# Softmax denominators of a cross-attention kernel: one of the probability sums moved to an accumulating transfer that GpSimd issues, VectorE summing all eight probability tiles, and ones products of half the width

## The chip, the cores and the metric

One core of one Trainium2 chip runs the whole kernel. The metric is the device time of one execution in microseconds (us), as the median over several executions. Durations below are from one execution that the hardware profiler recorded.

## The reference, cut to what matters

A cross-attention layer is followed by a gated expert layer, all in float32. There are 4 batches, 512 query rows, 1024 context rows and 16 heads of width 64:

```python
q = (lat @ Wq).reshape(b, n, HEADS, DHEAD).transpose(0, 2, 1, 3)
k, v = jnp.split(ctx @ Wkv, 2, axis=-1)            # then split in heads; k is rotated (rope)
attn = jnp.einsum('bhnd,bhsd->bhns', q, k) * scale
attn = jnp.clip(attn, -11.0, 11.0)
attn = jax.nn.softmax(attn, axis=-1)
out = jnp.einsum('bhns,bhsd->bhnd', attn, v)
x = x + (out.reshape(b, n, INNER) @ Wo + bo)
sel = jax.nn.sigmoid(jnp.einsum('bsd,ed->bse', xn, expert_sel))      # xn: normalised rows of x
scores = jax.nn.relu(jnp.einsum('bsd,edh->bseh', xn, keys))
x = x + jnp.einsum('bseh,ehv,bse->bsv', scores, values, sel)
```

The change is in how the sum over the 1024 context rows under the softmax is formed. The exponentials of a head pair stand in 8 tiles of 128 context rows each. The sum over the 8 tiles, and then over the 128 partitions, gives the denominators of 2 heads x 512 queries.

## The kernel before, in words

**Stages.** `attention_phase` handles 32 head pairs (4 batches x 8 pairs) one after another in a loop `for n in range(NPAIR): iteration(n)`, which each engine runs in its own order. `ffn_phase` then handles 4 chunks of 512 rows with 16 experts each. There is no scheduler: each engine's program is written out by hand, every instruction runs in the order written, and waits on semaphores join the engines.

**One iteration on each engine.** An iteration has 4 macro steps m = 0 to 3, each of two tiles of 128 context rows (s = 2m, 2m+1). TensorE writes the scores of a tile in one of two PSUM buffers (`scores`, L905), ScalarE takes the exponential into one of 4 buffers `probs` (`exp`, L1106), and VectorE clips it in place (`clip`, L1369). TensorE then multiplies it with the values (`attend`, L918). It runs two tiles behind within a pair, so that tiles 6 and 7 of pair n are attended in macro step 0 of iteration n+1. Between these come the projections of the next pair (keys, queries, values; all `product`, L149), the projection of the output of pairs before (`project_y`, L149), and for the first 22 iterations the normalising, turning and splitting of one more context tile.

**The denominators before.** After each macro step VectorE adds the two clipped tiles into `p_sum[m]` (`sum_up`, L1378, 128 x 1024 elements). In macro step 2 it adds `p_sum[0]` to `p_sum[1]` and in macro step 0 of the next iteration `p_sum[2]` to `p_sum[3]` (`sum_quad`, L1384). TensorE multiplies the two sums with a 128 x 32 tile of ones in four products of 512 columns (`denominators`, L931), each on 32 partitions of `side_ps`: two heads x two quad sums. ScalarE copies `o_ps` to `o_raw` (L1113; it first waits for `split_o`, L213, of the pair before) and then `side_ps` to `den` (L1117). SyncE turns four rows of `den` into `den_rows` (`turn_den`, L170). VectorE adds the two halves and inverts (`invert_den`, L177 and L179, in macro step 1), SyncE stores the result in memory (`store_inv`, L185) and loads it back spread over the partitions (`spread_inv`, L192), and VectorE scales `o_raw` (`scale_o`, L200, in macro step 2, just ahead of `sum_quad`).

**Order around the change.** SyncE's queue in iteration n is: `swap_k`, from n = 2 on `load_tile`, `turn_den(n-1)`, while n + 3 < 8 `load_weights(n+3)` (three transfers, L506 and L510), `store_inv(n-1)`, `spread_inv(n-1)`, and then the packs. `load_weights(n+3)` waits until the weights of pair n+2 have been split:

```python
def load_weights(w):
    wait(sp, w_split, w)
```

That split is GpSimd's `split_weights(n+2)` (L719 to L723) in iterations 0 to 5. GpSimd's order in iteration n before the change is: `rstd` (L682), `split_weights(n+2)`, in even iterations up to 2 `split_v_weights` and in iteration 0 also `split_first`, then `split_tile` (L702 to L709).

VectorE's order in macro step 1 is: normalise, clip, rope products, clip, `sum_up(n, 1)`, `split_q`, `invert_den`, `rope_add`. In macro step 2 it is: two clips, `add_y`, `sum_up(n, 2)`, `split_k`, `scale_o`, `sum_quad(n, 0)`. In the last iteration `sum_quad(n, 0)` follows `sum_up(n, 2)` directly, without the rope, key and query work between.

Of the kernel before, what the change touches and what calls it, by code (L numbers as in the profile page):

```python
# [74 lines left out]
def shared_state(nc, st):  # L75
# [26 lines left out]
    sh.den_rows = sb("den_rows", [P, 2, NQ // DH])  # L102
# [21 lines left out]
    sh.den_added = sem("den_added")  # L124
# [38 lines left out]
def turn_den(sp, sh, n):  # L163

    wait(sp, sh.den_evac, n + 1)
    for h in range(2):
        for e in range(2):
            at = DH * h + QUAD * e
            row = sh.den[at:at + 1, :].rearrange("a (p j) -> a p j", p=DH)
            sp.dma_start(sh.den_rows[DH * h:DH * h + DH, e, :], row).then_inc(sh.den_turned, DMA)  # L170


def invert_den(dve, sh, n):

    wait(dve, sh.den_turned, 4 * DMA * (n + 1))
    wait(dve, sh.inv_stored, DMA * n)
    dve.tensor_tensor(sh.inv_rows[:], sh.den_rows[:, 0, :], sh.den_rows[:, 1, :], ALU.add).then_inc(sh.den_added, 1)  # L177
    wait(dve, sh.den_added, n + 1)
    dve.reciprocal(sh.inv_rows[:], sh.inv_rows[:]).then_inc(sh.den_inv, 1)  # L179
# [86 lines left out]
def attention_phase(nc, sh, x, ctx_in, cosT, sinT, cols, Wq, Wkv, Wo, selT, keys, values, sel_dram, packs, v_packs,  # L266
                    inv_dram):
    with ExitStack() as st:
# [126 lines left out]
        quads_up = sem("quads_up")  # L395
        pv_done = sem("pv_done")
# [273 lines left out]
        def _(pool):  # L670
# [70 lines left out]

            def head_norm(t):
# [32 lines left out]
            def iteration(n):  # L775
                t, p = n + FIRST_TILES, n + 1
                if t < TILES:
                    rstd(t)
                if n + 2 < PAIRS:
                    split_weights(n + 2)  # L780
# [17 lines left out]
        def _(pe):  # L798
# [123 lines left out]
            def denominators(n):  # L922

                pe.wait_ge(quads_up, 2 * n + 2)
# [3 lines left out]
                for e in range(2):  # L928
                    for h in range(2):
                        at = DH * h + QUAD * e  # L930
                        mm = pe.matmul(side_ps[at:at + QUAD, :], ones[:], p_sum[2 * e + 1][:, h, :],  # L931
                                       start=True, stop=True)
# [109 lines left out]
        def _(act):  # L1042
# [65 lines left out]
            def evac_o(n):  # L1108
# [8 lines left out]
                act.copy(den[:], side_ps[:]).then_inc(den_evac, 1)  # L1117
# [93 lines left out]
        def _(dve):  # L1211
# [160 lines left out]
            def sum_up(n, m):  # L1372

                dve.wait_ge(clipped, STEPS * n + 2 * m + 2)
                if m % 2 == 1:
                    wait(dve, den_ready, n)
# [3 lines left out]
            def sum_quad(n, half):  # L1380

                dve.wait_ge(summed_up, MACROS * n + 2 * half + 2)
                first, second = p_sum[2 * half], p_sum[2 * half + 1]
                dve.tensor_tensor(second[:], first[:], second[:], ALU.add).then_inc(quads_up, 1)  # L1384
# [68 lines left out]
            def iteration(n):  # L1453
                p, t = n + 1, n + FIRST_TILES
                for m in range(MACROS):
# [17 lines left out]
                    if m == 0 and n > 0:  # L1473
                        sum_quad(n - 1, 1)
# [17 lines left out]
                    if m == 2:  # L1492
                        if last:
                            sum_quad(n, 0)
# [4 lines left out]
                        if not last:  # L1499
                            sum_quad(n, 0)  # L1500
# [12 lines left out]
            sum_quad(NPAIR - 1, 1)  # L1513
# [472 lines left out]
```

## Time and profile before

| | |
|---|---|
| median of 3 executions | 1025.62 us (1022.86 to 1027.14) |
| the profiled execution, its own time | 1021.78 us |
| its span in the profile | 1019.8 us |
| busy TensorE / VectorE / ScalarE / GpSimd | 95% / 81% / 50% / 25% |
| TensorE clock granted | 1.00 in every window read |
| attention iterations | 32, the denominators of the first at 67.7 us, of the last at 821.9 us |

The span is the time from the first to the last recorded instruction. An engine's busy time counts its instructions alone. TensorE's ends are modelled, so its stages are best read from start to start. The expert layer takes the time after some 825 us and is not touched, but for the denominators of pair 31, whose last steps lie in it.

### The profile page before, as it was taken

The page shows a single profiled execution, that of the slowest core. Times are in us where ns is not written, and L with a number is a line of the kernel's source. Part 1 is how long each engine was busy: PE and PEld are TensorE (multiplying, and loading weights), DVE is VectorE, ACT ScalarE, POOL GpSimd, SP SyncE. Part 2 cuts the span into 40 slices and gives each one's busy share as a digit, 9 for nine tenths or more (in the row PEclk, how much of TensorE's full clock was granted, in tenths as well). Part 3 has the DMA queues.
Part 4 walks back from the last instruction along what each step waited for, and adds up shares of the span by engine and source line. Part 5 has one row for each costly group of instructions (what it writes and reads, how often), then busy time and mean ns, then how long its engine had stood idle before and what let it go on. Part 6 is the DMA issues. An engine that isn't in the chain of part 4 may idle for free. (4 is left out here: it accounts for less than half of the span.)

```text
span 1019.8 us, 15953 instructions
## 1 busy us (share of the span) xinstructions
PE 973.5 (95%) x5688; PEld 618.8 (61%) x5688; DVE 827.5 (81%) x1234; ACT 513.6 (50%) x727; POOL 258.3 (25%) x228
## 2 busy tenths in 40 slices
PE   3989899999999999999999999999999879999998
PEld 2745455555555555555555555555555358888898
DVE  6699889999999999999999878989888876545322
ACT  4655555565556556566555555556555532222221
POOL 3354323121212121221312100321000135445443
PEclk9999999999999999999999999999999999999999
DMA  5643323332323232232333233233222481342331
GB/s 155 199 130 102 94 84 109 100 94 69 94 68 95 79 92 90 73 89 74 95 94 93 74 94 84 84 84 83 85 63 64 128 266 52 126 122 86 112 112 46
DMA packets 68953, 100.36 MB, mean 98 GB/s; under 512 B 21968, under 2 KB 44752, under 8 KB 66832
## 3 DMA queue, kind: packets, MB, share of 16 engines
q1 hardware_dynamic: 68880, 99.41, 32.7%
q8 instruction: 43, 0.70, 0.3%
q14 instruction: 30, 0.25, 0.1%
HBM read 70.01 MB, written 10.75 MB: 79 GB/s over the span
## 5 line engine op out<-in xcount | busy, mean ns | idle before, releaser
L1106 ACT ACTIVATE wide_a<-score_ps 128x1024 f32<-128x1024 f32 x256 | 249.0, 1028 | 119.8 <-PE score_ps L905 119.6
L1369 DVE TENSOR_SCALAR wide_a<-wide_a 128x1024 f32<-128x1024 f32 x256 | 188.6, 767 | 41.5 <-ACT wide_a L1106 41.5
L1378 DVE TENSOR_TENSOR p_sum<-wide_a 128x1024 f32<-128x1024 f32 x128 | 156.6, 1223 | 2.3
L918 PE MATMUL o_ps<-wide_a,v_sb 128*64 128x512 f32 x512 | 124.2, 605 | 4.6 <-issue 2.7
L918 PE MATMUL o_ps<-wide_a,values_a 128*64 128x512 f32 x512 | 124.0, 605 | 3.8 <-DVE wide_a L1369 2.1
L905 PE MATMUL score_ps<-q_hi,k_hi 64*128 64x512 f32 x512 | 114.6, 444 | 2.8 <-DVE k_lo L1348 2.1
L1881 DVE SCALAR_TENSOR_TENSOR act<-h_ps,wide_a 128x512 f32<-128x512 f32 x64 | 44.1, 690 | 89.2 <-PE h_ps L149 83.8
L905 PEld LDWEIGHTS score_ps<-q_hi,k_hi 64*128 64x128 f32 x512 | 47.8, 183 | 112.5 <-issue 75.0
L1807 ACT CAST act_hi<-act 128x512 fp32r<-128x512 f32 x64 | 39.8, 621 | 138.1 <-DVE act L1881 138.1
L1681 POOL TENSOR_TENSOR act_lo<-act,act_hi 128x512 fp32r<-128x512 f32 x64 | 84.8, 1326 | 95.8 <-ACT act_hi L1807 95.8
L905 PE MATMUL score_ps<-q_hi,k_lo 64*128 64x512 f32 x512 | 101.1, 391 | 0.0
L905 PE MATMUL score_ps<-q_lo,k_hi 64*128 64x512 f32 x512 | 100.4, 389 | 0.0
L702 POOL CAST wide_hi<-ctx_t 128x256 fp32r<-128x256 f32 x22 | 24.9, 1131 | 225.6 <-ACT x_t L1051 120.9
L1384 DVE TENSOR_TENSOR p_sum<-p_sum 128x1024 f32<-128x1024 f32 x64 | 80.5, 1257 | 0.0
L149 PE MATMUL out_ps<-val_hi,act_hi 128*128 128x256 f32 x256 | 72.9, 285 | 0.0
L149 PE MATMUL job_ps<-wv_hi,wide_hi 128*128 128x256 f32 x240 | 70.7, 295 | 1.4 <-ACT v_sb L1092 1.4
L149 PE MATMUL out_ps<-val_hi,act_lo 128*128 128x256 f32 x256 | 71.5, 279 | 0.0
L149 PE MATMUL out_ps<-val_lo,act_hi 128*128 128x256 f32 x256 | 71.5, 279 | 0.0
L918 PEld LDWEIGHTS o_ps<-wide_a,v_sb 128*64 128x64 f32 x512 | 31.2, 136 | 62.2 <-issue 54.5
L682 POOL TENSOR_TENSOR rstd_sb<-var_sb,power 128x2 f32<-128x2 f32 x22 | 22.9, 1041 | 178.8 <-DVE var_sb L1235 109.9
L918 PEld LDWEIGHTS o_ps<-wide_a,values_a 128*64 128x64 f32 x512 | 31.2, 136 | 60.2 <-issue 55.3
L149 PE MATMUL job_ps<-wv_lo,wide_hi 128*128 128x256 f32 x240 | 67.7, 282 | 0.0
(229 smaller groups left out, 2044.1 us busy)
## 6 DMA issues: line engine op xcount, KB each, us to landing
wide_a<-sel_dram SPq DMA_DIRECT2D x16, 1024.0 KB, 4.8
k_swap<-k SPq DMA_DIRECT2D x124, 128.0 KB, 2.3
w_hi<-packs_hi SPq DMA_DIRECT2D x26, 384.0 KB, 3.1
w_lo<-packs_lo SPq DMA_DIRECT2D x26, 384.0 KB, 3.7
den<-inv_dram SPq DMA_DIRECT2D x64, 128.0 KB, 2.9
ctx_raw<-ctx SPq DMA_DIRECT2D x24, 128.0 KB, 2.2
packs_hi<-w_hi SPq DMA_DIRECT2D x8, 384.0 KB, 3.2
packs_lo<-w_lo SPq DMA_DIRECT2D x8, 384.0 KB, 3.5
```

Of the source, the lines that this page charges most:

```text
L149: mm = pe.matmul(out, lhsT, rhs, start=start and i == 0, stop=stop and i == len(terms) - 1)
L682: pool.tensor_tensor(rstd_sb[slot][:], var_sb[slot][:], power[:, 0:2], ALU.pow).then_inc(rstd_ready, 1)
L702: pool.tensor_copy(ctx_at(ctxT_hi, t), ctx_t32[:]).then_inc(tile_hi, 1)
L905: mm = pe.matmul(score_ps[s % 2][:, h, :], k[par][rows, s * P:(s + 1) * P], q[par][rows, :], start=(i == 0), stop=(i == len(terms) - 1))
L918: mm = pe.matmul(o_ps[DH * h:DH * h + DH, :], v_sb[n // 2 % 2][:, at:at + DH], probs[s % RING][:, h, :], start=(s == 0), stop=(s == STEPS ...
L1106: act.activation(probs[s % RING][:], score_ps[s % 2][:], ACT.Exp, scale=DH ** -0.5).then_inc(exp_done, 1)
L1369: dve.tensor_scalar(probs[s % RING][:], probs[s % RING][:], CLIP_HI, CLIP_LO, ALU.min, ALU.max).then_inc(clipped, 1)
L1378: dve.tensor_tensor(p_sum[m][:], first, second, ALU.add).then_inc(summed_up, 1)
L1384: dve.tensor_tensor(second[:], first[:], second[:], ALU.add).then_inc(quads_up, 1)
L1681: pool.tensor_tensor(act_lo[e % ARING][:], act32[e % ARING][:], act_hi[e % ARING][:], ALU.subtract).then_inc(act_split, 1)
L1807: act.copy(act_hi[e % ARING][:], act32[e % ARING][:]).then_inc(act_hi_done, 1)
L1881: dve.scalar_tensor_tensor(out=act32[e % ARING][:], in0=h_ps[e % HRING][:], scalar=0.0, in1=gates[:, at:at + 512], op0=ALU.max, op1=ALU.mu ...
```

## The change

The sum of the first four tiles (`p_sum[0]` into `p_sum[1]`) leaves VectorE and becomes a transfer within SBUF that adds to its destination. GpSimd issues it, between `rstd` and `split_weights`. VectorE adds that sum to `p_sum[2]` where it added the first quad (`sum_six`), and the result to `p_sum[3]` where it added the second (`sum_all`). The ones products read one sum of eight tiles, each product 256 columns of it, and ScalarE copies 256 columns of `side_ps` in place of 512. The four transfers of `turn_den` each bring 256 elements to 32 partitions in place of 512 to 64, and `invert_den` has no addition left.

```diff
@@ turn_den
-            row = sh.den[at:at + 1, :].rearrange("a (p j) -> a p j", p=DH)
-            sp.dma_start(sh.den_rows[DH * h:DH * h + DH, e, :], row).then_inc(sh.den_turned, DMA)
+            row = sh.den[at:at + 1, 0:NQ // 2].rearrange("a (p j) -> a p j", p=QUAD)
+            sp.dma_start(sh.den_rows[at:at + QUAD, :], row).then_inc(sh.den_turned, DMA)
@@ invert_den
-    dve.tensor_tensor(sh.inv_rows[:], sh.den_rows[:, 0, :], sh.den_rows[:, 1, :], ALU.add).then_inc(sh.den_added, 1)
-    wait(dve, sh.den_added, n + 1)
-    dve.reciprocal(sh.inv_rows[:], sh.inv_rows[:]).then_inc(sh.den_inv, 1)
+    dve.reciprocal(sh.inv_rows[:], sh.den_rows[:]).then_inc(sh.den_inv, 1)
@@ gpsimd
+            def sum_four(n):
+
+                pool.wait_ge(summed_up, MACROS * n + 2)
+                pool.dma_start(p_sum[1][:], p_sum[0][:], accum_op=ALU.add).then_inc(quads_up, DMA)
@@ gpsimd, iteration
                 if t < TILES:
                     rstd(t)
+                sum_four(n)
                 if n + 2 < PAIRS:
                     split_weights(n + 2)
@@ denominators
-                pe.wait_ge(quads_up, 2 * n + 2)
+                pe.wait_ge(all_up, n + 1)
...
-                        mm = pe.matmul(side_ps[at:at + QUAD, :], ones[:], p_sum[2 * e + 1][:, h, :],
-                                       start=True, stop=True)
+                        mm = pe.matmul(side_ps[at:at + QUAD, 0:NQ // 2], ones[:],
+                                       p_sum[3][:, h, e * (NQ // 2):(e + 1) * (NQ // 2)], start=True, stop=True)
@@ evac_o
-                act.copy(den[:], side_ps[:]).then_inc(den_evac, 1)
+                act.copy(den[:, 0:NQ // 2], side_ps[:, 0:NQ // 2]).then_inc(den_evac, 1)
@@ vector
-                if m % 2 == 1:
+                if m == 3:
                     wait(dve, den_ready, n)
...
-            def sum_quad(n, half):
-
-                dve.wait_ge(summed_up, MACROS * n + 2 * half + 2)
-                first, second = p_sum[2 * half], p_sum[2 * half + 1]
-                dve.tensor_tensor(second[:], first[:], second[:], ALU.add).then_inc(quads_up, 1)
+            def sum_six(n):
+
+                dve.wait_ge(quads_up, DMA * (n + 1))
+                dve.wait_ge(summed_up, MACROS * n + 3)
+                dve.tensor_tensor(p_sum[2][:], p_sum[1][:], p_sum[2][:], ALU.add).then_inc(six_up, 1)
+
+            def sum_all(n):
+
+                dve.wait_ge(six_up, n + 1)
+                dve.wait_ge(summed_up, MACROS * n + 4)
+                dve.tensor_tensor(p_sum[3][:], p_sum[2][:], p_sum[3][:], ALU.add).then_inc(all_up, 1)
@@ vector, iteration (and after the loop)
-                        sum_quad(n - 1, 1)
+                        sum_all(n - 1)
...
-                            sum_quad(n, 0)
+                            sum_six(n)
```

## Rows read from the trace of the kernel before

**Rows 1.** Busy time by window; columns: window, PE, PEld, DVE, ACT, POOL, clock, DMA.
```profile
300.00:400.00 100.00, 100.00 (x578) 57.90 (x576) 92.43 (x133) 59.63 (x83) 18.11 (x16) 1.00 0.30 83
```

**Rows 2.** Timeline of TensorE around one pair's denominators; columns: start, us, engine, instruction.
```profile
414.00 1.94 PE L918 MATMUL o_ps<-wide_a,v_sb 128*64 128x512 f32 x8
415.86 1.06 PE L931 MATMUL side_ps<-p_sum,ones 128*32 128x512 f32 x8
416.86 0.50 PE L905 MATMUL score_ps<-q_hi,k_hi 64*128 64x512 f32 x2
```

**Rows 3.** Timeline of VectorE, one iteration, from the second sum_up on.
```profile
398.59 1.23 DVE L1378 TENSOR_TENSOR p_sum<-wide_a 128x1024 f32<-128x1024 f32 x1
...
400.56 0.16 DVE L177 TENSOR_TENSOR inv_rows<-den_rows 128x8 f32<-128x8 f32 x1
...
406.28 0.69 DVE L200 TENSOR_TENSOR o_raw<-o_raw,den 128x512 f32<-128x512 f32 x1 [0.17 <-DMA den<-inv_dram]
406.89 1.42 DVE L1384 TENSOR_TENSOR p_sum<-p_sum 128x1024 f32<-128x1024 f32 x1
...
416.64 0.68 DVE L213 TENSOR_TENSOR o_lo<-o_raw,o_hi 128x512 fp32r<-128x512 f32 x1
...
419.45 0.69 DVE L1369 TENSOR_SCALAR wide_a<-wide_a 128x1024 f32<-128x1024 f32 x1 [1.05 <-ACT wide_a L1106]
```

**Rows 4.** Timeline of ScalarE in the same iteration, between VectorE's split and clip.
```profile
417.41 0.59 ACT L1113 COPY o_raw<-o_ps 128x512 f32<-128x512 f32 x1 [2.72 <-DVE o_lo L213]
...
417.89 0.59 ACT L1117 COPY den<-side_ps 128x512 f32<-128x512 f32 x1
...
418.37 1.96 ACT L1106 ACTIVATE wide_a<-score_ps 128x1024 f32<-128x1024 f32 x2
```

**Rows 5.** Groups by line and form: a ScalarE copy of double width.
```profile
L1098 ACT CAST k_hi<-k 128x1024 fp32r<-128x1024 f32 x31 | 32.6, 1051 | 42.9 <-DVE k L1343 42.9
```

**Rows 6.** Timeline of GpSimd in iteration 1: the weight split.
```profile
70.82 0.19 POOL L719 TENSOR_TENSOR carry_pool<-power 128x2 f32<-128x2 f32 x1
...
72.06 2.36 POOL L723 TENSOR_TENSOR w_lo<-w_raw,w_hi 128x768 fp32r<-128x768 f32 x1
```

**Rows 7.** Timeline of SyncE's queue in iteration 1, from the weight loads on.
```profile
74.44 0.39 SPq L506 DMA_DIRECT2D w_raw<-Wq  x1
...
75.39 0.47 SPq L510 DMA_DIRECT2D w_raw<-Wo  x1
79.44 0.34 SPq L185 DMA_DIRECT2D inv_dram<-inv_rows  x1
80.86 1.11 SPq L192 DMA_DIRECT2D den<-inv_dram  x2
```

**Rows 8.** Timeline of VectorE in iterations 1 and 2.
```profile
77.27 1.23 DVE L1378 TENSOR_TENSOR p_sum<-wide_a 128x1024 f32<-128x1024 f32 x1
...
84.24 0.69 DVE L200 TENSOR_TENSOR o_raw<-o_raw,den 128x512 f32<-128x512 f32 x1
...
97.27 2.02 DVE L1369 TENSOR_SCALAR wide_a<-wide_a 128x1024 f32<-128x1024 f32 x1 [0.30 <-ACT wide_a L1106]
...
103.72 1.23 DVE L1378 TENSOR_TENSOR p_sum<-wide_a 128x1024 f32<-128x1024 f32 x1
...
112.78 0.96 DVE L200 TENSOR_TENSOR o_raw<-o_raw,den 128x512 f32<-128x512 f32 x1 [1.70 <-DMA den<-inv_dram]
```

**Rows 9.** Transfers by line; columns: count, KB each, median us from issue to landing.
```profile
wide_a<-sel_dram SPq DMA_DIRECT2D x16, 1024.0 KB, 4.8
...
den<-inv_dram SPq DMA_DIRECT2D x64, 128.0 KB, 2.9
...
y_tile<-yT SPq DMA_DIRECT2D x2, 512.0 KB, 5.0
```

**Rows 10.** Timeline of VectorE in the last iteration.
```profile
808.07 1.23 DVE L1378 TENSOR_TENSOR p_sum<-wide_a 128x1024 f32<-128x1024 f32 x1
...
814.60 1.22 DVE L1384 TENSOR_TENSOR p_sum<-p_sum 128x1024 f32<-128x1024 f32 x1
```

More of the change, by code:

```diff
@@ L101, in shared_state @@
     sh.den = sb("den", [P, NQ])
-    sh.den_rows = sb("den_rows", [P, 2, NQ // DH])
+    sh.den_rows = sb("den_rows", [P, NQ // DH])
     sh.inv_rows = sb("inv_rows", [P, NQ // DH])
@@ L123, in shared_state @@
     sh.den_turned = sem("den_turned")
-    sh.den_added = sem("den_added")
     sh.den_inv = sem("den_inv")
@@ L395, in attention_phase @@
         quads_up = sem("quads_up")
+        six_up = sem("six_up")
+        all_up = sem("all_up")
         pv_done = sem("pv_done")
@@ L1499, in iteration @@
                         if not last:
-                            sum_quad(n, 0)
+                            sum_six(n)
                         if n == 29:
@@ L1512, in _ @@
                 iteration(n)
-            sum_quad(NPAIR - 1, 1)
+            sum_all(NPAIR - 1)
             split_o(dve, sh, NPAIR - 2, 0)
```

## The prediction, made before the changed kernel was built

> **What bounds the kernel now.** I read the busy time by window first. In the 32 attention iterations TensorE is busy all the time and VectorE 92% [rows 1], so a pair costs about what TensorE needs for it, some 24.2 us, and VectorE has little to give. The timelines say how little. VectorE's split of the output ends at 417.32 us, ScalarE copies `o_ps`, then `side_ps`, then takes the next exponential, each directly behind the one before, and VectorE's clip starts when that exponential is done [rows 3, 4]. ScalarE's 2.72 us wait ahead of it ends with VectorE's split, not with TensorE. So there are two loops of nearly the same length: TensorE's own stream, and VectorE with a hop over ScalarE and back. A saving counts only if it shortens both, and a wait put on VectorE counts at once. TensorE alone has a cushion: the second quad sum ends about 1.1 us ahead of the ones products.
>
> **The change part by part.** The sum is made against the profiled execution, 1021.8 us, which is 3.8 below the median of the runs shown; the forecast adds that back. Here T is the end of `sum_up(n, 1)`, from which the new transfer hangs.
>
> *Ones products.* They take 1.00 us from start to start (415.86 to 416.86) [rows 2]. The eight instructions of two attends before them take 1.86, or 0.93 for four of the same 512 columns, so about 0.07 to 0.14 us of the 1.00 belongs to loading and starting, not to columns. Halving the rest saves 0.43 us a pair. The bounds are 0 (instructions, not columns, set it) and 0.50.
>
> *The VectorE loop.* `invert_den` loses its addition, 0.16 us [rows 3]. The copy of `den` halves: 512 columns are 0.59 us, 1024 are 1.05 [rows 4, 5], so 256 are about 0.36, and 0.23 goes. With the pause between addition and reciprocal that is about 0.42 us of this loop, close to what TensorE saves. Both loops shrink alike: 32 x 0.42 = 13.4 us gained. The lighter `turn_den` transfers are off the path, since `invert_den` finds them landed, and count nothing; were the cover gone they would save a few tenths. VectorE's additions of 1024 elements stay two per pair: its two quad sums are replaced by two others, in the same places. No VectorE time is freed by the transfer itself.
>
> *The transfer, in ordinary iterations.* No accumulating transfer and none issued by GpSimd is in this trace. Its issue is bounded by SyncE's 0.39 [rows 7] and a long GpSimd instruction, 2.36 [rows 6]; I take 1.0. The landing: 128 KB takes 2.9, 1024 KB 4.8 us [rows 9], so 512 KB more costs about 1.1 us. Adding reads source and destination, 1024 KB in all, so I take 4.8. The lower bound is that of 128 KB, 2.9; the upper is twice the 512 KB copy inside SBUF, 2 x 5.0 [rows 9]. It lands at T + 5.8, bounds T + 3.3 and T + 12.4. `sum_six` stands where the quad sum is now, at 406.89, with T = 399.82: T + 7.1 [rows 3]. By itself the transfer would just be hidden. But `scale_o` comes ahead of it in VectorE's order, at T + 6.5, and already waits 0.17 us for the spread inverse. That spread is issued about T + 2.4 [rows 7, 8], in the middle of the new transfer, on the same DMA engines. Sharing them puts it off by 0.5 to 1.1 us. I take 0.4 us of new waiting per iteration, mean over those with some slack and those with none, and 27 iterations: +10.8 us. Bounds: 0, and 3.9 per iteration (lower issue cost, upper landing).
>
> The Trainium skill's page "DMA: Bandwidth & Descriptors" (Anatomy of one DMA) gives about 2.0 us plus bytes over 436 GB/s; with the reads doubled that is 4.4 us as an estimate, 0.4 shorter than my landing. No run here shows it, and the sum would be a few microseconds lower by it.
>
> *The first iterations.* This is the part of the price that rows carry best. `sum_four` stands ahead of `split_weights` in GpSimd's order, and its wait holds that split until T. Behind the split waits SyncE: its load of the next weights is issued at 74.44, as the split ends (72.06 + 2.36) [rows 6, 7], and behind that load in the same queue stand `store_inv` and `spread_inv`, for which VectorE's `scale_o` waits. Before, the split was over by T (78.50) [rows 8]. After, the chain from T is: issue 1.0, split 3.6 (70.82 to 74.42), three loads 1.42 (74.44 to 75.86), store to spread 1.42 (79.44 to 80.86) [rows 7], and some 3.5 until the second spread part has landed (0.55 to its issue, 2.9 to land), 10.9 in all. `scale_o` starts at T + 5.7 in iteration 1 and T + 7.8 in iteration 2 [rows 8]. It would be 5.2 and 3.1 us late, 4.1 on average. It happens in iterations 1 to 4, where `load_weights(n+3)` exists: 16.6 us of VectorE's time. What is queued behind `scale_o` is `sum_six`, the clips of tiles 6 and 7 and the sum the ones products need, so TensorE stops with it, beyond its cushion. Against this stands that the split no longer runs beside the clip in macro step 1, which took 2.02 us beside it where 0.69 is usual [rows 3, 8]: 1.33 us back in each of iterations 2 to 5, 5.3 in all. About 1 us more per stalled iteration is hidden in the new wait, since GpSimd's work then meets an idle VectorE: 4. Net +7.3 us, between 0 (all absorbed) and +16. The transfer counts nothing extra here, as `scale_o` is later than it. Iteration 0 and iteration 5 only move GpSimd work that nobody waits for soon.
>
> *The last iteration.* `sum_six` follows T (809.30) already at T + 5.3 (814.60) [rows 10], and large loads of values end just then. I take a landing at T + 7.8: +2.5 us, between 0 and 7.
>
> *Sum:* -13.4 + 10.8 + 7.3 + 2.5 = +7.2. On the profiled execution 1029.0; on the median 1032.8, so 1033 us.
>
> **The rivals.** A change of 0.5%, 5.1 us, is about what a measurement of this kernel can tell from none.
>
> *A, forecast: the transfer and the spread inverse crowd each other, and the early queue stalls.* 1026 to 1042 us. For it: `scale_o` waits for the spread 0.17 and 1.70 us already [rows 3, 8]. Chance 0.36.
>
> *B, everything hidden.* The transfer lands before T + 6.5, the spread is not put off, and most of the early stall is absorbed (net 2). Then -13.4 + 2 = -11.4: 1014, or up to 1019 with a little waiting left. For it: T + 5.8 is ahead of T + 7.1, and DMA engines are 30% busy [rows 1]. Against it: VectorE has no slack in its loop. Place: `scale_o` in macro step 2; it decides once the spread lands less than 0.3 us later than now. Chance 0.24.
>
> *C, the adding transfer is slow.* If adding on the way halves the rate again, it lands at about T + 8.5 and VectorE waits 1.4 us at `sum_six`, 27 times: +38 in place of 10.8, about 1060 us. VectorE's loop, now 25.2 us long, would be the bound and TensorE would wait at the ones products. Decides from T + 7.1 on. Chance 0.22.
>
> *D, hidden in ordinary iterations, full price in the first ones.* -13.4 + 7.3 + 1 = -5.1: 1020.5. Chance 0.10, half of it counted as faster.
>
> *E, GpSimd cannot issue beside VectorE's clips.* If issuing lasts beyond T + 2.1, two clips of together 1.3 us stand in its way, as GpSimd's split and a clip now lengthen each other (2.02 against 0.69) [rows 3, 8]. The landing moves to about T + 8.4: near 1057 us. The Trainium skill's page "SBUF — State Buffer" (Who interferes with whom) says that VectorE in a two-port mode locks GpSimd out, descriptor writing included; by that rule this rival is real, and the clip beside the split agrees with the lock itself. Chance 0.08.
>
> That the ones products gain nothing from fewer columns is possible too. The VectorE loop would still shrink, but TensorE's would not, and 13 us would be missing from each case: it sits in the range.
>
> **How the numbers follow.** Likeliest is A, 1033. Faster by over 0.5%: B and half of D, 0.29. Slower: C, E and two thirds of A, 0.54. Within: the rest, 0.17. The range reaches from B's lower part, 1015, to between C and the slowest transfers, 1063, leaving out the lowest of B and the top of C. A's own range is 1026 to 1042.
>
> **What would show it.** TensorE: ones products near 0.57 us from start to start. ScalarE: the copy of `den` near 0.36. VectorE, iterations 1 to 4: `scale_o` about 10 to 11 us behind T, waiting for the spread, and SyncE's weight loads ahead of it at T + 4.6. Ordinary iterations: a wait ahead of `scale_o` for `den`, little at `sum_six`; under C or E the wait is at `sum_six`, for the transfer. The landing time of that transfer, near 4.8 us, decides between A and C. The forecast is wrong if `scale_o` starts no later than now (B), or if `sum_six` waits over 1 us (C or E).

## The result and the profile after

The changed kernel is slower: 1046.18 us (median of 4, 1044.43 to 1048.36) against 1025.99 us (1022.86 to 1027.14), a ratio of 1.0209, with a 95% interval of 1.0182 to 1.0236. The forecast was 1033 in a range of 1015 to 1063. The sign and the range held; the loss is 20 us where 7 were forecast. The profiled execution spans 1042.5 us (before 1019.8).

Lines of the page of the changed kernel: busy times, the granted clock in 40 slices, the new transfer's issue, and transfers with KB and us to landing.

```profile
PE 972.6 (93%) x5688; PEld 626.4 (60%) x5688; DVE 818.5 (79%) x1202; ACT 508.3 (49%) x727; POOL 270.8 (26%) x260
...
PEclk9989998999999999999999999999999999999999
...
L744 POOL DMA_DIRECT2D p_sum<-p_sum x32 | 29.2, 913 | 330.3 <-DVE p_sum L1383 324.4
...
p_sum<-p_sum POOLq DMA_DIRECT2D x32, 512.0 KB, 5.0
...
den<-inv_dram SPq DMA_DIRECT2D x64, 128.0 KB, 3.6
```

The issue takes 0.91 us (forecast 1.0), the landing 5.0 us (forecast 4.8; 4.4 by the estimate from the Trainium skill's page "DMA: Bandwidth & Descriptors"). The spread of the inverse lands after 3.6 us, 2.9 before [rows 9]. Next the ones products on TensorE, and a group of the view by line, the copy of `den` on ScalarE:

```profile
403.38 1.94 PE L923 MATMUL o_ps<-wide_a,values_a 128*64 128x512 f32 x8
405.25 0.64 PE L936 MATMUL side_ps<-p_sum,ones 128*32 128x256 f32 x8
405.81 0.50 PE L910 MATMUL score_ps<-q_hi,k_hi 64*128 64x512 f32 x2
```

```profile
L1122 ACT COPY den<-side_ps 128x256 f32<-128x256 f32 x32 | 12.1, 377 | 2.4 <-PE side_ps L936 2.4
```

From start to start the ones products take 0.56 us (forecast 0.57; 1.00 in [rows 2]), the copy 0.38 (0.36; 0.59 in [rows 4]). Now the waits of the changed kernel, with their sum, number and longest:

```profile
DVE o_raw L197 <- DMA den<-inv_dram: 41.4, 28, 5.1
...
PEld side_ps L936 <- DVE p_sum L1395: 31.9, 18, 3.8
```

Before, `scale_o` waited 4.9 us in all. `sum_six` does not appear with a wait for the transfer: VectorE waits for the spread, not for the sum. That is rival A's picture.

**Where the time went.** The starts of the ones products mark the pairs. First the changed kernel, pairs 0, 4, 23, 25 and 31, then the kernel before.

```profile
70.11 1.05 PE L936 MATMUL side_ps<-p_sum,ones 128*32 128x256 f32 x8 [1.97 <-DVE p_sum L1395]
...
186.07 0.64 PE L936 MATMUL side_ps<-p_sum,ones 128*32 128x256 f32 x8 [0.97 <-DVE p_sum L1395]
...
645.00 0.64 PE L936 MATMUL side_ps<-p_sum,ones 128*32 128x256 f32 x8 [0.49 <-DVE p_sum L1395]
...
694.90 0.64 PE L936 MATMUL side_ps<-p_sum,ones 128*32 128x256 f32 x8
...
845.49 0.64 PE L936 MATMUL side_ps<-p_sum,ones 128*32 128x256 f32 x8 [1.51 <-DVE p_sum L1395]
```

```profile
67.74 1.06 PE L931 MATMUL side_ps<-p_sum,ones 128*32 128x512 f32 x8 [0.75 <-DVE p_sum L1384]
...
172.10 1.07 PE L931 MATMUL side_ps<-p_sum,ones 128*32 128x512 f32 x8 [0.48 <-DVE p_sum L1384]
...
632.95 1.07 PE L931 MATMUL side_ps<-p_sum,ones 128*32 128x512 f32 x8
...
682.49 1.06 PE L931 MATMUL side_ps<-p_sum,ones 128*32 128x512 f32 x8
...
821.93 1.06 PE L931 MATMUL side_ps<-p_sum,ones 128*32 128x512 f32 x8 [1.44 <-DVE p_sum L1384]
```

The differences of such rows, for these two and for the experiments below, in us. The step from pair k to k+1 is mostly the time of iteration k+1.

| kernel | to pair 0 | 0 to 4 | 4 to 23 | 23 to 25 | 25 to 31 |
|---|---|---|---|---|---|
| before | 67.7 | 104.4 | 460.9 | 49.5 | 139.4 |
| after | 70.1 | 116.0 | 458.9 | 49.9 | 150.6 |
| splits_first | 68.3 | 104.3 | 457.7 | 50.4 | 151.8 |
| store_before_loads | 70.8 | 104.8 | 457.9 | 55.6 | 150.6 |
| no_transfer | 68.1 | 103.2 | 453.1 | 49.8 | 136.9 |
| no_transfer_wide | 69.2 | 102.1 | 460.4 | 49.6 | 138.8 |
| plain_copy | 70.2 | 118.4 | 459.8 | 52.0 | 146.1 |
| vector_adds | 69.1 | 108.1 | 470.8 | 52.4 | 144.5 |
| after_store | 68.8 | 110.0 | 470.2 | 53.1 | 152.9 |
| after_reciprocal | 67.9 | 105.7 | 470.2 | 54.6 | 149.3 |
| late_scale | 68.4 | 101.8 | 452.0 | 50.9 | 142.1 |
| before_late_scale | 67.9 | 101.2 | 460.7 | 49.6 | 143.2 |
| late_scale_head | 68.0 | 101.5 | 452.1 | 48.7 | 139.1 |

So in the 19 pairs from 4 to 23 the changed kernel is ahead by 1.9 us. It loses 14.0 us up to pair 4 and 11.2 us from pair 25 on. The first loss was forecast, at half its size; the second was not. Nor is the price of the transfer in the 19 middle pairs even: of the 4.6 us between splits_first and no_transfer there, 3.3 fall on four pairs (10 to 12 and 18 to 20). In iterations 10, 11, 18 and 19 of the changed kernel `scale_o` waits 1.7 to 2.0 us, and these are, among iterations 5 to 26, just those in which the DMA view shows a packet of the instruction queue (q8) between the store of the inverse and its use. The spread then lands after 4.4 us in place of 3.6.

**The early loss.** Iteration 1 of the changed kernel: GpSimd, SyncE's queue, VectorE.

```profile
79.12 0.93 POOL L744 DMA_DIRECT2D p_sum<-p_sum  x1 [5.88 <-PE job_ps L148]
...
81.25 2.70 POOL L722 TENSOR_TENSOR w_lo<-w_raw,w_hi 128x768 fp32r<-128x768 f32 x1
```

```profile
83.97 0.39 SPq L505 DMA_DIRECT2D w_raw<-Wq  x1
...
84.92 0.47 SPq L509 DMA_DIRECT2D w_raw<-Wo  x1
85.81 0.34 SPq L182 DMA_DIRECT2D inv_dram<-inv_rows  x1
87.81 1.76 SPq L189 DMA_DIRECT2D den<-inv_dram  x2
```

```profile
77.59 1.23 DVE L1383 TENSOR_TENSOR p_sum<-wide_a 128x1024 f32<-128x1024 f32 x1
...
82.18 2.92 DVE L1374 TENSOR_SCALAR wide_a<-wide_a 128x1024 f32<-128x1024 f32 x2
...
91.95 0.69 DVE L197 TENSOR_TENSOR o_raw<-o_raw,den 128x512 f32<-128x512 f32 x1 [4.26 <-DMA den<-inv_dram]
```

T is 78.82. The split ends at 83.95, the load goes out 0.02 us later, behind it the store and the spread; `scale_o` starts at T + 13.1 (before T + 5.7 [rows 8]). In iterations 2 to 4 it is T + 13.1, 12.1 and 11.7, where it was T + 7.8, 7.7 and 6.0.

**The late loss.** An ordinary iteration of the changed kernel (13, of those with the shortest wait), then iteration 26, each with GpSimd's issue of the transfer, SyncE's store and spread, and VectorE.

```profile
390.00 0.89 POOL L744 DMA_DIRECT2D p_sum<-p_sum  x1 [6.46 <-DVE p_sum L1383]
```

```profile
390.44 0.33 SPq L182 DMA_DIRECT2D inv_dram<-inv_rows  x1
391.86 1.67 SPq L189 DMA_DIRECT2D den<-inv_dram  x2
```

```profile
395.94 0.98 DVE L197 TENSOR_TENSOR o_raw<-o_raw,den 128x512 f32<-128x512 f32 x1 [0.17 <-DMA den<-inv_dram]
```

```profile
702.91 0.93 POOL L744 DMA_DIRECT2D p_sum<-p_sum  x1 [6.11 <-DVE p_sum L1383]
712.15 3.30 POOL L758 TENSOR_TENSOR wide_lo<-w_raw,wide_hi 128x1024 fp32r<-128x1024 f32 x1 [8.31 <-ACT wide_hi L1167]
```

```profile
703.66 0.33 SPq L182 DMA_DIRECT2D inv_dram<-inv_rows  x1
707.80 1.12 SPq L189 DMA_DIRECT2D den<-inv_dram  x2
```

```profile
702.83 0.69 DVE L1337 TENSOR_TENSOR q_lo<-job_ps,q_hi 128x512 fp32r<-128x512 f32 x1 [0.22 <-ACT q_hi L1090]
...
711.40 0.69 DVE L197 TENSOR_TENSOR o_raw<-o_raw,den 128x512 f32<-128x512 f32 x1 [2.55 <-DMA den<-inv_dram]
...
713.14 3.46 DVE L1374 TENSOR_SCALAR wide_a<-wide_a 128x1024 f32<-128x1024 f32 x2
...
717.78 0.68 DVE L1456 TENSOR_TENSOR xT_lo<-job_ps,xT_hi 128x512 fp32r<-128x512 f32 x1
```

The spread can be issued when the store has landed. Ordinarily the store goes out 0.44 us after GpSimd's issue has begun, and the spread follows 1.42 us later. In iteration 26 it goes out 0.75 us after it, since VectorE waited for ScalarE's `q_hi` ahead of the reciprocal, and the spread follows only 4.14 us later. In iterations 5 to 31 of this trace, stores that go out up to 0.46 us behind the start of GpSimd's issue take 1.4, and those of iterations 23 and 26 to 29, 0.68 to 1.01 behind it, take 3.8 to 4.5. Except in iteration 27, each of these slow stores is done 4.75 to 4.89 us after GpSimd's issue has begun, about when the transfer itself lands (5.0). So `scale_o` comes 2.55 us late, the two clips behind it fall beside GpSimd's split of the expert keys and take 3.46 us, and only then comes the split of the head's rows, `xT_lo`. In the kernel before, the head's rows were split first and the clips that met GpSimd, 2.90 us for two, came behind it. TensorE, in its timeline:

```profile
713.80 0.40 PE L148 MATMUL side_ps<-o_hi,w_lo 128*128 128x512 f32 x1
718.61 0.64 PE L148 MATMUL job_ps<-wide_hi,w_hi 128*128 128x512 f32 x1 [4.41 <-DVE xT_lo L1456]
719.05 0.63 PE L148 MATMUL job_ps<-wide_lo,w_hi 128*128 128x512 f32 x1
...
722.56 0.39 PE L148 MATMUL job_ps<-wide_lo,w_hi 128*128 128x512 f32 x1
```

It waits 4.41 us, and then eight matmuls follow each other at 0.43 us, until 722.0, and the next at 0.23. Eight times 0.20 are 1.6 us; with the wait that is 6.0, an estimate of the loss, and the pair takes 30.1 where it took 24.3. The granted clock is 1.00 from 700 to 710, 0.94 from 710 to 720 and 0.89 from 720 to 730 us: for about 3.4 us TensorE has the lower of its levels, 1.2 GHz. The two stretches with losses show the same in the view by window (columns as in [rows 1]), where before it was 1.00 in each:

```profile
51.00:200.00 149.00, 128.46 (x700) 72.39 (x698) 123.39 (x156) 73.03 (x106) 58.42 (x60) 0.93 0.42 112
200.00:640.00 440.00, 434.14 (x2535) 253.10 (x2534) 393.89 (x552) 255.30 (x358) 80.70 (x85) 1.00 0.41 107
640.00:850.00 210.00, 189.84 (x1059) 105.74 (x1058) 174.00 (x217) 105.63 (x138) 26.06 (x18) 0.98 0.43 115
```

### The profile page after: what moved, and what is told of

Its sections match the earlier page's. It is cut to its first block and busy times, and to the rows that moved or that the text cites. A ratio compares the mean times of both kernels' runs of the same rounds, so it can differ in the third digit from the quotient of the medians.

```text
span 1042.5 us, 15986 instructions
## 1 busy us (share of the span) xinstructions
PE 972.6 (93%) x5688; PEld 626.4 (60%) x5688; DVE 818.5 (79%) x1202; ACT 508.3 (49%) x727; POOL 270.8 (26%) x260
## 5 line engine op out<-in xcount | busy, mean ns | idle before, releaser
L1374 DVE TENSOR_SCALAR wide_a<-wide_a 128x1024 f32<-128x1024 f32 x256 | 185.7, 755 | 37.3 <-ACT wide_a L1111 37.3
L1383 DVE TENSOR_TENSOR p_sum<-wide_a 128x1024 f32<-128x1024 f32 x128 | 159.6, 1247 | 2.3
L910 PE MATMUL score_ps<-q_hi,k_hi 64*128 64x512 f32 x512 | 117.1, 453 | 4.7 <-DVE k_lo L1353 4.0
L744 POOL DMA_DIRECT2D p_sum<-p_sum x32 | 29.2, 913 | 330.3 <-DVE p_sum L1383 324.4
L910 PE MATMUL score_ps<-q_hi,k_lo 64*128 64x512 f32 x512 | 103.5, 399 | 0.0
L910 PE MATMUL score_ps<-q_lo,k_hi 64*128 64x512 f32 x512 | 102.7, 396 | 0.0
L1118 ACT COPY o_raw<-o_ps 128x512 f32<-128x512 f32 x32 | 18.8, 587 | 104.2 <-DVE o_lo L210 97.7
```

Of the source, the lines that this page charges most:

```text
L744: pool.dma_start(p_sum[1][:], p_sum[0][:], accum_op=ALU.add).then_inc(quads_up, DMA)
L910: mm = pe.matmul(score_ps[s % 2][:, h, :], k[par][rows, s * P:(s + 1) * P], q[par][rows, :], start=(i == 0), stop=(i == len(terms) - 1))
L1118: act.copy(o_raw[:], o_ps[:]).then_inc(o_evac, 1)
L1374: dve.tensor_scalar(probs[s % RING][:], probs[s % RING][:], CLIP_HI, CLIP_LO, ALU.min, ALU.max).then_inc(clipped, 1)
L1383: dve.tensor_tensor(p_sum[m][:], first, second, ALU.add).then_inc(summed_up, 1)
```

## The experiments

The theory: the transfer itself is nearly hidden; what costs is where it stands in GpSimd's order (early), and that the inverse's way through memory meets it (late and ordinary). The rivals: adding on the way makes it slow; GpSimd's issue is slow; the gain was not there. Each expectation stands as it was written before its run. Ratios are to the kernel before in the same series, with the 95% interval.

**1. splits_first.** GpSimd's weight splits go ahead of the transfer, as they stood before.

```diff
-                sum_four(n)
                 if n + 2 < PAIRS:
                     split_weights(n + 2)
                 if n % 2 == 0 and n // 2 + 2 < DUOS:
                     split_v_weights(n // 2 + 2)
+                sum_four(n)
```

> The changed kernel with GpSimd's transfer issued behind the weight splits of the iteration instead of ahead of them; only iterations 0 to 5 differ. Theory (order in GpSimd's queue): the first four periods between ones products, 28.5, 30.1, 28.6 and 28.7 us in the changed kernel, fall to 24 to 26, scale_o starts at most 8 us behind T, and the clock granted from 51 to 200 us returns to 1.00; the time falls by 12 to 16 us, to about 1032. Rival (DMA traffic of the transfer makes the early stall): the periods stay above 27.5 and the time falls by less than 4.

1032.06 us, 1.0081 (1.0059 to 1.0104), as expected. The early loss is gone: 104.3 us from pair 0 to 4, clock 1.00 in that stretch (one period, 27.8 us, stays long, as in the kernel before with 28.2). The late one is not. GpSimd, then SyncE, in iteration 1, where `scale_o` now starts at 85.48, T + 6.4:

```profile
72.66 2.37 POOL L722 TENSOR_TENSOR w_lo<-w_raw,w_hi 128x768 fp32r<-128x768 f32 x1
79.43 0.92 POOL L744 DMA_DIRECT2D p_sum<-p_sum  x1 [4.39 <-DVE p_sum L1383]
```

```profile
75.06 0.39 SPq L505 DMA_DIRECT2D w_raw<-Wq  x1
...
79.85 0.34 SPq L182 DMA_DIRECT2D inv_dram<-inv_rows  x1
81.28 1.71 SPq L189 DMA_DIRECT2D den<-inv_dram  x2
```

**2. store_before_loads.** The changed kernel with the other end of the chain cut: SyncE's store and spread go ahead of the weight loads, GpSimd's order stays.

```diff
-                if n + 3 < PAIRS:
-                    load_weights(n + 3)
                 if n > 0:
                     store_inv(sp, sh, inv_dram, n - 1)
                     spread_inv(sp, sh, inv_dram, n - 1)
+                if n + 3 < PAIRS:
+                    load_weights(n + 3)
```

> The changed kernel with its GpSimd order kept (transfer ahead of the weight splits), and in SyncE's queue the store and the spread of the inverse ahead of the weight loads of the iteration instead of behind them. Theory (the early stall is a chain through SyncE's queue: transfer, split, loads, store, spread): cutting it here cures it as well as moving the transfer did; scale_o starts at T + 6 to 8 us in iterations 1 to 4, the clock from 51 to 200 us is at 1.00, and the time is 10 to 14 us below the changed kernel, about 1033. Rival (GpSimd's split beside VectorE's work in macro step 2 costs the time itself): the first four periods stay above 27.5 and the time falls by less than 5.

1036.43 us, 1.0121 (1.0093 to 1.0150), some 3 us more than expected. In iterations 1 to 5 `scale_o` has no wait (it starts at T + 7.9 to 8.9, a little later than expected), the clock is 0.98 from 51 to 200, and pair 0 to 4 takes 104.8 us: it was SyncE's order that carried GpSimd's delay to VectorE. What keeps it behind splits_first in the profiles is the start (70.8 us) and the late stretch, where one more iteration, 25, has a slow store (3.82 us, issued 1.01 us behind the transfer). Pair 23 to 24 also grows to 28.1 us though its store takes 1.42. There VectorE waits 2.68 us for `k_swap` at the start of the iteration, TensorE then 2.34 us for the head's `x_head`, and eight of its matmuls follow at 0.43 us. (In no_transfer VectorE waits for `k_swap` there too, 2.13 us; why was not traced.)

**3. no_transfer.** Without the transfer and the wait for it; tiles 0 and 1 are left out of the sum.

```diff
-                sum_four(n)
...
-                dve.wait_ge(quads_up, DMA * (n + 1))
```

> The changed kernel without the transfer and without the wait for it; VectorE still makes its two additions of 1024 elements, so tiles 0 and 1 are left out of the denominators. Theory (the gain is real, all of the loss hangs on the transfer): steady periods near 23.8, the late periods of 30.1 and 27.8 us go back to 25, scale_o waits under 6 us in all, and the time is 10 to 14 us below the kernel before, about 1013. Rival (narrower ones products gain nothing because VectorE's loop is the bound): within 4 us of the kernel before.

1009.88 us, 0.9866 (0.9817 to 0.9915). The gain that the change is after is real: 13.2 us, with an interval of some 9 to 19. The waits of `scale_o` come to 4.8 us, as before, and the late loss is gone (136.9 us, stores of 1.4 us in iterations 23 to 27): it hangs on the transfer.

**4. no_transfer_wide.** The same with ones products of 512 columns; tiles 0 and 1 are left out, and the four products give other sums than the reference.

```diff
-                        mm = pe.matmul(side_ps[at:at + QUAD, 0:NQ // 2], ones[:],
-                                       p_sum[3][:, h, e * (NQ // 2):(e + 1) * (NQ // 2)], start=True, stop=True)
+                        mm = pe.matmul(side_ps[at:at + QUAD, :], ones[:], p_sum[3][:, h, :],
+                                       start=True, stop=True)
```

> no_transfer with ones products of 512 columns as in the kernel before (the four products, the copy of den stays at 256 columns). Theory (TensorE's stream sets the steady period): steady periods go from 23.74 back to about 24.1 and the time up by 10 to 13 us against no_transfer, to about 1021. Rival (VectorE's loop sets it): within 3 us of no_transfer.

1019.10 us, 0.9960 (0.9942 to 0.9978). A pair takes 24.23 us (460.4 / 19) where it takes 23.85 with half the columns, so columns set it: 0.38 us a pair, 9 us in all, a little under the 10 to 13 expected. What is left, with VectorE's shorter loop, is 3.5 us ahead of the kernel before, and only 0.5 of it in the 19 middle pairs. Narrow products with VectorE's old, longer loop were not run.

**5. vector_adds.** The third addition stays on VectorE, ahead of `sum_six`, without the transfer.

```diff
-                sum_four(n)
...
-                dve.wait_ge(quads_up, DMA * (n + 1))
+                dve.wait_ge(summed_up, MACROS * n + 2)
+                dve.tensor_tensor(p_sum[1][:], p_sum[0][:], p_sum[1][:], ALU.add).then_inc(quads_up, 1)
+                dve.wait_ge(quads_up, n + 1)
```

> The changed kernel without the transfer, the first addition made by VectorE just ahead of its second, so a third addition of 1.2 us per pair on VectorE; the output is whole. Theory (VectorE's loop has no slack): the period of steady iterations is 23.8 + 1.2 = 25.0, the time about 1035 to 1042, some 25 us above the kernel with no transfer. Rival (the pause before the ones products absorbs it): below 1022.

1045.32 us, 1.0205 (1.0162 to 1.0249), 3 us above the expected range: no better than the transfer. A pair takes 24.78 us, 0.93 more than without the addition (23.85), though the addition lasts 1.22. VectorE has about 0.3 us to spare in a pair, and no room for a third addition. Pairs 23 to 24 and 25 to 26 grow to 27.5 and 27.4 us here, with no transfer and stores of 1.4 us: in that stretch any lateness of VectorE is dear, not this transfer's alone.

**6. plain_copy.** The transfer copies and does not add; tiles 2 and 3 are left out.

```diff
-                pool.dma_start(p_sum[1][:], p_sum[0][:], accum_op=ALU.add).then_inc(quads_up, DMA)
+                pool.dma_start(p_sum[1][:], p_sum[0][:]).then_inc(quads_up, DMA)
```

> The changed kernel with a plain copy of the same 512 KB in place of the adding transfer; tiles 2 and 3 are left out of the denominators. If reading the destination as well is what crowds the spread inverse: the landing falls from 5.0 to about 3.9 us, the waits ahead of scale_o in iterations 6 to 22 fall to near nothing, and the time falls by 5 to 8 us. If the order of the two in the DMA queues is what counts, and not the bytes: the long store-to-spread times of about 4.1 us in iterations 23 and 26 to 29 stay, the early stalls stay, and the time falls by less than 4.

1045.42 us, 1.0202 (1.0160 to 1.0245), as slow as with the addition, though the transfer is faster. Neither expectation came true as written: the time did not fall, and the stores of iterations 26, 28 and 29 take 2.1 to 2.5 us, not 4. From its page:

```profile
L744 POOL DMA_DIRECT2D p_sum<-p_sum x32 | 18.9, 591 | 329.1 <-DVE p_sum L1383 323.2
...
p_sum<-p_sum POOLq DMA_DIRECT2D x32, 512.0 KB, 3.0
```

Adding costs 2.0 us of landing and 0.3 us of issue, and in the sum neither decides: from pair 25 on the copy is 4.5 us cheaper, up to it 5.5 us dearer. In place of the 1.42 the store now takes 2.75 us in nearly every iteration, at the same 0.44 us behind GpSimd's issue, and `scale_o` waits 48.8 us in all. A slow store is done 3.1 to 3.3 us after that issue has begun in 24 of iterations 5 to 30, and the copy lands after 3.0: here too the two end together. The price is the meeting, not the addition; another size than 512 KB was not tried.

**7. after_store.** splits_first, and GpSimd issues the transfer when the store has landed.

```diff
                 pool.wait_ge(summed_up, MACROS * n + 2)
+                wait(pool, sh.inv_stored, DMA * n)
```

> splits_first with GpSimd waiting, before it issues the transfer, until the stored inverse of the pair before has landed. Theory (the store is long when it is issued behind the transfer's data, 1.4 against 4.1 us): every store-to-spread time is at 1.4, also in iterations 26 to 29, whose periods fall to 25; the transfer starts some 2 us later, so sum_six waits up to 1 us per pair, and the spread meets more of it. Time 1022 to 1034. Rival (late iterations are long for another reason, their own transfers): the store times of about 4 us stay in iterations 26 to 29.

1055.47 us, 1.0309 (1.0279 to 1.0339), 21 us above the expected range. The stores take 1.4 us in all but iterations 2, 3 and 27 (3.13, 3.44 and 2.00, where the kernel before, which has no such transfer, has 3.37, 3.34 and 2.34). But the transfer now starts at T + 2.7, lands after 5.8 us, and `sum_six` waits for it. The periods of iterations 26 and 27 stay at 30.9 and 27.5 us: a fast store alone does not cure them while VectorE waits elsewhere. From the waits:

```profile
DVE p_sum L1390 <- DMA p_sum<-p_sum: 39.0, 27, 2.5
```

This is rival C's picture, brought about by a late start. The landing at T + 5.3 in the changed kernel leaves 1.8 us until `sum_six` at T + 7.1, and a start 2.4 us later, with a landing 0.8 us slower, uses them up.

**8. after_reciprocal.** The same with an earlier release, when the reciprocal is done.

```diff
                 pool.wait_ge(summed_up, MACROS * n + 2)
+                wait(pool, sh.den_inv, n)
```

> splits_first with GpSimd waiting, before it issues the transfer, until VectorE's reciprocal of the pair before is done: some 0.1 us later than now in steady iterations, 0.5 us later in iterations 26 to 29. Theory (a store of the inverse issued more than about 0.5 us behind GpSimd's issue takes 4 us in place of 1.4, since the transfer's data are ahead of it): all stores are at 1.4, the waits ahead of scale_o in iterations 26 to 29 fall from 2.4 to under 1 us, the period of 28.1 us falls to about 25, and the time is 6 to 10 us below splits_first. Rival (those iterations are slow whatever the store does): within 3 us of splits_first.

1047.51 us, 1.0226 (1.0195 to 1.0257), 15 us above splits_first where 6 to 10 below it were expected. The transfer starts at T + 1.27, 0.5 us behind the store, and the stores take 1.4 us, but for those of iterations 2, 3 and 27 (3.59, 2.96 and 1.95). Now the spread pays: from iteration 5 to 30 it is 5.1 to 6.9 us from its issue to `scale_o`, where it was 4.1 to 5.8 in the changed kernel's iterations with a fast store from 6 to 30. Its landing, from the page:

```profile
den<-inv_dram SPq DMA_DIRECT2D x64, 128.0 KB, 5.1
```

A shift of a microsecond or two only chooses who pays: the store (when it goes out later), the spread (here), or `sum_six` (after_store).

**9. late_scale and before_late_scale.** `scale_o` moves behind the two clips of macro step 3, on splits_first and on the kernel before.

```diff
-                        if n > 0 and not last:
-                            scale_o(dve, sh, n - 1)
...
+                    if m == 3 and n > 0 and not last:
+                        scale_o(dve, sh, n - 1)
                     sum_up(n, m)
```

> splits_first with VectorE's scale_o moved from macro step 2 to macro step 3, behind the two clips there; output whole. Theory (what is left of the loss, 22 us against the kernel with no transfer, is the wait for the spread inverse, 29.8 us in splits_first): the wait ahead of scale_o falls below 4 us in all, the periods of 30.5 and 28.1 us (iterations 26 and 27) fall to 25, and the time to 1011 to 1016, ahead of the kernel before by 8 us or more. Rival (the transfer itself is late at sum_six, hidden so far behind scale_o): sum_six waits 0.5 to 1 us per pair in place of it and the time stays above 1022.

> The kernel before with the same move of scale_o alone. It has 4.9 us of waits ahead of scale_o in all, so by the theory it gains 0 to 4 us; if it gains 8 or more, late_scale owes its time to the move and not to the change.

1013.22 us, 0.9889 (0.9865 to 0.9913), and 1021.71 us, 0.9980 (0.9963 to 0.9997). With the change the move is worth 19 us, without it 0.9: nothing is wrong with the transfer once nobody waits for the inverse. `scale_o` has no wait left, `sum_six` 1.5 us in all, and pairs 4 to 23 take 452.0 us, no more than without the transfer. The 0.9 is a sum of two larger parts: against the kernel before, before_late_scale gains 3.1 us from pair 0 to 4 and loses 3.8 from pair 25 on. One pair, 25 to 26, is still long, 27.98 us, and with the move alone it is 28.45 (before 24.31), so transfer or not. In both traces `scale_o`, put ahead, moves the sum of two tiles beside GpSimd's split of the keys, where it takes 3.41 us in place of 1.23. Behind it comes the split of the head's rows, TensorE waits 2.3 us for it, and then eight or so of its matmuls follow at 0.43 us.

**10. late_scale_head.** So from iteration 24 on `scale_o` goes behind the head's work, at the end of macro step 3.

```diff
-                    if m == 3 and n > 0 and not last:
+                    if m == 3 and 0 < n < 24:
                         scale_o(dve, sh, n - 1)
...
                             head_split_x(2 * (n - 26))
+                        if n >= 24 and not last:
+                            scale_o(dve, sh, n - 1)
```

> late_scale with scale_o of iterations 24 on put further back, behind the work for the expert layer's first rows in macro step 3. Theory (in iteration 26 TensorE waits for head_split_x, which stands behind scale_o and beside GpSimd's split of the keys, and then runs at a lower granted clock): the period of 28.0 us falls to 25 and the time by 2 to 4 us against late_scale, to about 1010. Rival (the split of the keys alone makes that period): no change beyond 1 us.

1010.66 us, 0.9870 (0.9845 to 0.9895), the lowest median of a kernel that computes the whole output; its interval overlaps that of late_scale, so that the step between them rests on the traces. Pair 25 to 26 takes 24.23 us. The stores of iterations 29 to 31 still take 4.0 to 4.2 us; only what waits has changed. The kernel before with `scale_o` placed in this way was not run. As an estimate, before_late_scale without the 4.1 us of its one long pair would be at pair 31 after 818.5 us, and this kernel is there after 809.4, so that some 9 us would be left to the change. The waits of `scale_o`:

```profile
DVE o_raw L197 <- DMA den<-inv_dram: 0.9, 1, 0.9
```

## Why the prediction was off

**Ones products and VectorE's loop: right.** -13.4 forecast; no_transfer gives -13.2 (1009.88 - 1023.04), 0.41 us a pair from 4 to 23 (460.9 - 453.1, over 19). That TensorE's loop had to shrink is shown: the wide products give back 9 of it. That VectorE's had to is only estimated: the third addition leaves it 0.3 us to spare in a pair, so without its forecast 0.42 about 0.1 us a pair would be missing.

**The transfer in ordinary iterations: the mechanism right, the size too large.** The landing of 5.0 was forecast at 4.8, the wait was put at `scale_o` for the spread, and there it is. But splits_first is 4.6 us behind no_transfer from pair 4 to 23, 0.24 us a pair, where 0.4 was taken. For 27 pairs that is 6.5 us in place of 10.8 (and there are 26: iteration 0 has no `scale_o`). The mean hides that most of it falls on four pairs. VectorE's few tenths of slack may have taken the rest.

**The first iterations: the mechanism right, the size too small, and this is one of the two errors.** +7.3 was forecast; after against splits_first it is 1.8 + 11.7 = 13.5 us up to pair 4. The step that failed is the chain "10.9 in all": it is 12.5 in the mean. In iteration 1 the split ends at T + 5.1 in place of 4.6 (its last instruction is 2.70 us beside VectorE's clips, where I had taken [rows 6] with 2.36 beside a rope product), loads and a gap take 1.9 in place of 1.42, store to spread 2.00 in place of 1.42, and the rest 4.1 in place of 3.5. The durations were read one by one in iteration 1 of the kernel before, where the work fell beside other neighbours. That they vary was there to be read: in iterations 2 and 3 of that same trace store to spread takes 3.37 and 3.34. The lateness over four iterations comes to 7.4 + 5.3 + 4.4 + 5.7 = 22.8 us, against 16.6. Pair 0 to 4 lost 11.7 of it, so 11.1 were absorbed, where I had set 9.3 against it (5.3 + 4), though not quite as I had put it: the collision of clip and split was not taken away but moved, and the two clips at 82.18 take 2.92 us beside the split where 1.28 is usual. The iteration 0 that "nobody waits for soon" lost 1.8 us. That TensorE ran at the lower clock after its waits was not foreseen at all. Its share was not separated, but a granted clock of 0.93 over 149 us is an estimated 10 us of full clock lost, some of them while TensorE stood still anyway.

**The late iterations: missing from the forecast, the other error.** "Ordinary iterations" took all from 5 to 30 for alike, with a mean wait. From pair 25 to 31 the changed kernel loses 11.2 us to before and 13.7 to no_transfer. Two things were readable in the trace before and were not read: that VectorE's next product in the head iterations stands behind `scale_o` and feeds TensorE without a cushion, and that GpSimd's key split stands beside the clips there. The third could not be read in full: the store of the inverse, which I had left at 1.42 us, depends on how far it stands behind the new transfer. In place of the +10.8 and +2.5 for iterations 5 to 31, the changed kernel lost 19.6 us to no_transfer from pair 4 to 31.

**The last iteration: right by chance.** +2.5 was put on a wait at `sum_six`. There is none; the last two pairs lose 0.4 and 1.3 us, and in the last one two clips take 3.90 us beside GpSimd's split, where it was 1.25. The split stands behind the transfer in GpSimd's order and starts at T + 0.85, where it started 0.3 us ahead of T.

**The rivals.** B fell: the landing at T + 5.3 would have been early enough for `sum_six`, but the spread was put off. C fell: `sum_six` has no wait, and plain_copy, which lands 2 us earlier, is no faster in the sum. E fell: the issue takes 0.91 us in the mean. D is half true: the ordinary iterations cost little, and at pair 25 splits_first is 1.8 us ahead of the kernel before; but the first ones cost twice their price, and the late ones stood in no rival. That the ones products gain nothing fell with 0.56 us.

The sum as measured at the ones products of pair 31, all against the profiled executions: -10.8 (no_transfer against before, of the 13.4), +13.5 for the order early, +5.9 for the transfer up to pair 23 (splits_first against no_transfer), +1.2 for what the changed kernel has more than splits_first in between, +13.8 from pair 23 on: 23.6 = 845.5 - 821.9.

What stays open: how much of the early loss is the lower clock and how much the wait itself; why a store issued up to 0.52 us behind the transfer gets past it and a later one does not; what the instruction queue's packet does to its neighbours; and whether each execution loses by the same stores (one trace of each kernel was read; of the five with an adding transfer released by T, all have a slow store in iteration 29, and all but late_scale_head in 27 and 28).

## What to carry to other kernels

When an instruction gets a new wait, follow every queue behind it to its end, and price the chain with the range that its durations have over all iterations, not with one reading of each. Don't average over iterations that differ in what stands behind the wait: read one iteration of each kind, the ramp and the tail too. When an added transfer turns out to cost more than its own time, look whether its neighbour, a small transfer that others wait for, can be given slack by moving its reader; that was worth 19 us here, more than the change's whole gain.

## What the hardware showed that I had not expected

- A small store to memory on SyncE's queue takes 1.4 us when it is issued up to 0.52 us after the issue of a 512 KB adding transfer within SBUF has begun on GpSimd's queue, and 3.5 to 4.5 us when 0.65 us or more after it. So it stands in iterations 5 to 31 of five traces (after, splits_first, store_before_loads, late_scale, late_scale_head), with 25 slow stores, the one in iteration 1 of store_before_loads (1.32 us behind) among them, and one in between (2.08 us at 0.44). Of the 25, 19 are done 4.75 to 4.89 us after that issue began, and the transfer lands after 5.0. Behind a plain copy it is 2.75 us at 0.44, and 2.1 to 2.5 at 0.75 to 0.99: again done with the transfer, which lands after 3.0. The new transfer is not the only cause of a slow store: in iterations 2 and 3 of the kernel before, which has none, it takes 3.37 and 3.34 us, and in iteration 3 of splits_first 3.63 at 0.43.
- The instruction queue (q8 in the DMA view) moves a packet between store and use of the inverse in iterations 10, 11, 18, 19, 27 and 31 of the kernel before and of the changed one, and in 1 of both and 2 and 3 of the kernel before. All slow stores of the kernel before (2.3 to 3.4 us, in 2, 3, 27 and 31) fall on such iterations. In the changed kernel the spread lands after 4.4 to 4.5 us in 10, 11, 18 and 19, and after 3.6 to 3.9 in the ones between.
- A transfer of 512 KB within SBUF lands after 5.0 us if it adds and after 3.0 if it copies; issuing takes GpSimd 0.91 and 0.59 us in the mean.
- The Trainium skill's page "SBUF — State Buffer" (Who interferes with whom) has VectorE, in a two-port mode, lock GpSimd out, descriptor writing included. In this trace the issue shows no such delay in the mean (0.91 us). In after_reciprocal, where it starts 1 us later and runs into two clips, it takes 1.22 us in nearly every iteration, with clips no longer than usual (1.29): 0.3 us more, not their whole length. What the changed kernel's trace does show is clips and GpSimd's splits lengthening each other, 3.46 us for two clips beside a split of 3.30, where two take 1.28.
- After a wait of 4.41 us (the changed kernel), and already after waits of 2.3 us (store_before_loads, late_scale, before_late_scale), some eight of TensorE's matmuls stood 0.43 us apart in place of 0.23. In the early stretch of the changed kernel, with waits of 1.4 to 2.9 us, the granted clock from 51 to 200 us was 0.93 where it had been 1.00.
